# Who writes the attention mask into PSUM: two matmuls or one ScalarE copy

## What is computed

```python
q = l2norm(q) * qs; k = l2norm(k) * ksc           # then rotary tables on q and k
mask = (it < jb) | (it > jb + w) | (jb == -1)
sim = jnp.einsum('bhwie,bhwje->bhwij', bq, bk2) * QK_SCALE
sim = jnp.where(mask, -jnp.finfo(sim.dtype).max, sim)
attn = jax.nn.softmax(sim, -1)
out = jnp.einsum('bhwij,bhwje->bhwie', attn, bv2)
...
x = attn_layer(shift_tokens(x), ...) + x
x = ffn_layer(shift_tokens(x), ...) + x           # a * gelu(gate) @ W2 + b2
```

## Time and profile before

| | us |
|---|---|
| median of 3 runs | 3832.99 (3829.45 to 3838.61) |
| profiled execution, its own time | 3835.11 |
| its span, first to last instruction | 3833.3 |
| PE busy | 3290.7 (86%) |
| DVE busy | 2808.5 (73%) |
| ACT busy | 2595.7 (68%) |
| POOL busy | 2500.6 (65%) |

### The profile page before, as it was taken

One profiled execution on the slowest core, in us unless ns is written; L12 is line 12 of the kernel. 1 busy time (PEld: TensorE's weight loads), 2 busy tenths in 40 slices (PEclk: granted clock), 3 DMA queues, 4 the chain that ended last, 5 costly groups with the idle time before them and its releaser, 6 DMA issues.

```text
span 3833.3 us, 127009 instructions
## 1 busy us (share of the span) xinstructions
PE 3290.7 (86%) x52864; PEld 2810.5 (73%) x53056; DVE 2808.5 (73%) x4272; ACT 2595.7 (68%) x3787; POOL 2500.6 (65%) x2289
## 2 busy tenths in 40 slices
PE   3444448999989999899999899999999998999996
PEld 2333236888878888788888788888787887888885
DVE  5766766777777777777777777777777777777772
ACT  2222225777777777777777777777777776777774
POOL 1000007777777877777777777778777777787771
PEclk7666668999999999999999999999999999999997
DMA  1000001111111111111111111111111111111111
GB/s 56 0 0 0 0 0 35 50 41 35 35 29 40 56 34 35 35 41 41 47 35 35 34 37 59 35 35 35 35 37 55 35 35 31 41 37 30 36 34 31
DMA packets 54643, 130.05 MB, mean 34 GB/s; under 512 B 10944, under 2 KB 28864, under 8 KB 53312
## 3 DMA queue, kind: packets, MB, share of 16 engines
q1 hardware_dynamic: 54080, 122.02, 10.9%
HBM read 19.25 MB, written 2.10 MB: 6 GB/s over the span
## 4 chain that ended last, share of the span: by engine, by line
PE 72%; ACT 12%; DVE 7%; issue 7%; POOL 1%; DMA 0%; SPq 0%; ACTq 0%; DVEq 0%; POOLq 0%
PE pair L217 58%; PE pair L220 14%; ACT qT L737 7%; ACT sq L727 2%; DVE qT L362 1%; ACT ss L732 0%; DVE VA L347 0%; DVE qT L353 0%; DVE wq_l L843 0%; ACT qT L275 0%; DVE tab L835 0%; ACT qT L272 0%; DVE VB L358 0%; DVE qT L326 0%; DVE qT L316 0%
## 5 line engine op out<-in xcount | busy, mean ns | idle before, releaser
L966 POOL TENSOR_TENSOR qk<-qk,ts 128x1024 f32<-128x1024 f32 x384 | 914.8, 2383 | 312.2 <-DVE ts L857 293.4
L945 POOL TENSOR_TENSOR qk<-qk,rn 128x1024 f32<-128x1024 f32 x384 | 729.3, 1921 | 43.1 <-issue 28.3
L853 DVE TENSOR_TENSOR qk<-pair,tab 128x1024 f32<-128x1024 f32 x384 | 468.6, 1220 | 373.0 <-ACT sq L719 370.3
L217 PE MATMUL pair<-wq_h,xs_h 128*128 128x512 f32 x1152 | 515.2, 447 | 34.7 <-issue 15.0
L220 PE MATMUL pair<-small,qk 128*128 128x128 f32 x3192 | 452.5, 285 | 66.7 <-ACT qT L737 49.4
L714 ACT ACTIVATE Sx<-Sx 128x1024 f32<-128x1024 f32 x192 | 203.7, 1061 | 413.9 <-DVE Sx L870 413.9
L220 PEld LDWEIGHTS pair<-small,qk 128*128 128x128 f32 x3192 | 361.0, 146 | 151.3 <-issue 127.5
L857 DVE TENSOR_TENSOR ts<-pair,tab 128x1024 f32<-128x1024 f32 x384 | 466.5, 1215 | 0.0
L217 PE MATMUL pair<-wq_h,xs_l 128*128 128x512 f32 x1152 | 464.8, 403 | 0.0
L861 DVE TENSOR_REDUCE ss<-sq 128x16 f32<-128x1024 f32 x384 | 464.3, 1209 | 0.0
L217 PE MATMUL pair<-wq_l,xs_h 128*128 128x512 f32 x1152 | 460.8, 400 | 0.0
(11 more groups left out here) (204 smaller groups left out, 6959.1 us busy)
## 6 DMA issues: line engine op xcount, KB each, us to landing
VB<-VA SPq DMA_DIRECT2D x192, 384.0 KB, 3.5
VB<-VA SPq DMA_DIRECT2D x96, 128.0 KB, 3.4
wq_raw<-wqkv SPq DMA_DIRECT2D x6, 1536.0 KB, 8.8
xf<-xT SPq DMA_DIRECT2D x96, 64.0 KB, 1.9
xf<-xT SPq DMA_DIRECT2D x96, 63.8 KB, 2.0
wo_sb<-wo SPq DMA_DIRECT2D x6, 512.0 KB, 3.6
out<-X SPq DMA_DIRECT2D x8, 256.0 KB, 2.3
w_raw<-fw SPq DMA_DIRECT2D x6, 341.0 KB, 8.0
```

The source lines that it names most:

```text
L217: return T_.matmul(out, lhsT, rhs, start=start, stop=stop, **k)
L853: V_.tensor_tensor(h3(qk[:, now, kind, :], DH), h3(source[:, :], DH), rep(tab[:, 2 * kind, b, :], HEADS, DH), ALU.mult)
L945: G_.tensor_tensor(x, x, bc(rn[:, then, kind * HEADS:(kind + 1) * HEADS], HEADS, DH), ALU.mult).then_inc(S["scaled"], 1)
L966: G_.tensor_tensor(qk[:, now, kind, :], qk[:, now, kind, :], ts[:, kind, :], ALU.add).then_inc(S["added"], 1)
```

## The change

The bf16 mask, the bf16 identity, and the two VectorE casts that made them are gone. TensorE no longer waits for `o_kept` ahead of the scores and issues no mask matmuls; it waits for a new semaphore `masked`. ScalarE, right behind the copy of oT and ahead of the copy of kT, waits for `o_kept` and copies the f32 mask from SBUF, repeated for 8 head pairs, over all of PB. The scores still accumulate (start flag off). For that, the write flags in PB have to be set when they come: of the product of P and V only the first matmul of each bank and partition half starts a group, so that all columns are left written. At step 1, before any such product, two ordinary matmuls write PB for the same end.

```diff
-        mask_bf = sb("mask_bf", [P, BLOCKS, PAIRS * 2 * KEYS], BF16)
-        ident_bf = sb("ident_bf", [P, P], BF16)
...
                                 last = mm(PB[odd * DH:(odd + 1) * DH, to:to + WIN],
-                                          values[rows, ring, head * DH:(head + 1) * DH], PT[rows, a, q0:q0 + WIN])
+                                          values[rows, ring, head * DH:(head + 1) * DH], PT[rows, a, q0:q0 + WIN],
+                                          a == 0 and w == 0, True, skip_group_check=True)
...
             if pl.has(1):
-                if pl.has(3):
-                    e.wait_ge(S["o_kept"], blocks(pl, "o_kept", 3, 1))
                 bb = (t - 1) % BLOCKS
-                for u in range(2):
-                    mm(PB[:, u * UNIT:(u + 1) * UNIT], ident_bf[:, :], mask_bf[:, bb, u * UNIT:(u + 1) * UNIT], True, False, skip_group_check=True)
+                if t == 1:
+                    for u in range(2):
+                        last = mm(PB[:, u * UNIT:(u + 1) * UNIT], xs_h[:, 0, 0:P], wq_h[:, 0:UNIT])
+                    last.then_inc(S["opened"], 1)
+                e.wait_ge(S["masked"], blocks(pl, "masked", 1, 1))
                 e.wait_ge(S["qkT_kept"], blocks(pl, "qkT_kept", 1, 2))
...
             if pl.has(1):
+                bb = (t - 1) % BLOCKS
+                if pl.has(3):
+                    e.wait_ge(S["o_kept"], blocks(pl, "o_kept", 3, 1))
+                elif pl.has(2):
+                    e.wait_ge(S["shifted"], blocks(pl, "shifted", 2, 1))
+                else:
+                    e.wait_ge(S["opened"], 1)
+                A_.activation(h3(PB[:, :], P), rep(mask[:, bb * P:(bb + 1) * P], PAIRS, P), ACT.Copy).then_inc(S["masked"], 1)
                 e.wait_ge(S["qkT_done"], blocks(pl, "qkT_done", 1, 2))
-                bb = (t - 1) % BLOCKS
                 A_.activation(kT[:, :, WIN + bb * P:WIN + (bb + 1) * P], h3(PC[:, :], P), ACT.Copy).then_inc(S["qkT_kept"], 1)
...
             dve.wait_ge(S["loaded"], 64)
-            V_.tensor_copy(mask_bf[:, :, :].rearrange("p b (a k) -> p b a k", k=2 * KEYS),
-                           mask.rearrange("p (b o k) -> p b o k", b=BLOCKS, o=1).broadcast_to([P, BLOCKS, PAIRS, 2 * KEYS]))
-            V_.tensor_copy(ident_bf[:, :], ident)
             stage1(dve, stage1_dve)
```

More of the change, by code:

```diff
@@ L8 @@
 I32 = mybir.dt.int32
-BF16 = mybir.dt.bfloat16
 ALU = mybir.AluOpType
@@ L143, in build @@
             "seeded": 1, "newton": 3, "normed": 1, "added": 2, "scaled": 2, "qkT_done": 2, "qkT_kept": 2, "s_done": 1,
-            "maxed": 1, "shifted": 1, "exp_done": 1, "rows_summed": 1, "inverted": 1, "weighed": 1, "pT_done": 1,
+            "maxed": 1, "masked": 1, "shifted": 1, "exp_done": 1, "rows_summed": 1, "inverted": 1, "weighed": 1, "pT_done": 1,
             "pT_kept": 1, "av_done": 1, "o_kept": 1, "y_done": 1, "x_updated": 1, "v_kept": 1,
@@ L154, in build @@
         S = {n: sem(n) for n in (*STEP, *PER_SEQ, *LOADS, *PARTS, "xf0", "xf1", "vb0", "vb1", "vb2", "vb3", "phase", "loaded",
-                                 "stored", "lane0", "lane1", "lane2", "lane3", "o_copied", "o_t", "o_sum", "zeroed",
+                                 "stored", "lane0", "lane1", "lane2", "lane3", "opened", "o_copied", "o_t", "o_sum", "zeroed",
                                  "cleared", "waited")}
```

## The result

| | before | after |
|---|---|---|
| median, us | 3832.99 (5 runs) | 3856.45 (3849.24 to 3858.59, 5 runs) |
| ratio, 95% interval | | 1.0065 (1.0045 to 1.0084) |
| profiled execution, us | 3835.11 | 3849.24 |
| its span, us | 3833.3 | 3847.4 |

The forecast was 3825, with a range of 3806 to 3856.

What follows compares the result with a forecast made beforehand. The prediction took TensorE to bound the kernel: -84.5 us for the mask matmuls, +74 for odd-step stalls and +2 at layer boundaries gave about -8, so a median of 3825 us, range 3806 to 3856.

Steps and rivals of the forecast that it cites:

- What bounds the kernel: TensorE, 86% busy and 72% of the chain of waits; time taken from it counts wherever nothing else is as late.
- The odd step: Late kT copy stalls TensorE 0.76 us at the `xf` transposes, against 0.44 saved; 74 us of stalls over 94 steps.
- The even step: kT's delay is hidden at W1's third part; the 0.44 us saved is kept, narrowly, with slacks of 0.10 and 0.16.
- The second rival: ScalarE's chain from value copy to maximum bounds the even step too; at a 1.3 us mask copy 3861; chance 0.09.
- a chance of gain only: Shorter mask copy, or stalls absorbed where TensorE's issue idles let it catch up; about 3808 us; chance 0.15.
- the third rival: TensorE's clock falls after the odd step's new stall; 1.7 us in one step of four, 41 us, 3866; chance 0.13.
- The sum: Whole kernel: -84.5 for the mask matmuls, +74 for odd-step stalls, +2 at layer boundaries, giving -8.5 us.

Runs made afterwards that it cites:

- nomask: Changed kernel without any mask, neither matmuls nor ScalarE copy, so the mask is left out of the computation; 3762.24 us, ratio 0.9828.
- both: Kernel before with the ScalarE mask copy added and the mask matmuls kept; 3904.98 us, ratio 1.0215.
- swap_after: Changed kernel with the W2 product placed ahead of the `xf` transposes on TensorE; 3779.58 us, ratio 0.9866.
- kt_odd: Changed kernel with the mask copy behind the copy of kT in odd steps, ahead of it in even steps; 3783.86 us, ratio 0.9874.
- gelu64_after: Changed kernel with the three gelus cut to 64 of 256 columns and one memset more at the start; 3838.59 us, ratio 1.0025.
- even_act: Even steps as in the change (ScalarE writes the mask), odd steps as in the kernel before (two matmuls); 3825.57 us, ratio 0.9994.
- odd_act: Odd steps as in the change (ScalarE writes the mask), even steps as in the kernel before (two matmuls); 3882.72 us, ratio 1.0148.
- after_pad: Changed kernel with four semaphore increments per step on TensorE in place of the mask matmuls and their weight loads; 3862.31 us, ratio 1.0079.
- kt_first: Changed kernel with the mask copy behind the copy of kT in both kinds of step; 3792.04 us, ratio 0.9906.
- before_pad16: Kernel before with 16 semaphore increments per step on TensorE ahead of the mask matmuls; 3967.23 us, ratio 1.0355.

## Why the prediction was wrong, step by step

**What bounds the kernel:** right for the part that holds the mask matmuls, worth 0.44 us in each step (nomask: -0.43 and -0.43). It was not TensorE's path throughout: between the scores and the transposes of Q the path runs through VectorE and ScalarE, by 0.10 us, which the chain with its 72% for TensorE doesn't show. The even step failed on that piece.

**The odd step:** right. Predicted +0.32 (0.76 stalled, 0.44 saved), measured +0.34 in the median, with a stall of 0.75. Over 94 steps 74 us were predicted and 67 measured, since some steps have little or no stall. The runs both, swap_after and kt_odd show the cause: it is that kT comes late for the `xf` transposes, and nothing else of the copy.

**The even step:** this is the step that failed. The prediction said that "the even step's 0.44 is kept, narrowly", after it had checked two users of the delayed chain, the transposes of P and the square of K. The third, the transposes of Q behind the copy of P, had a slack of nothing. Measured -0.30. The term was -42 us and is -29: 13 us, which gelu64_after gives back (15.70, -15 to -18 us). The subtraction behind the maximum came 0.30 earlier against the 0.18 worked out for the maximum; with 0.18 the loss would have been larger still. The second rival named this chain, but let it decide only from a mask copy of 1.19 us. It decided at 1.03.

**What was not priced:** 15 us above the medians, in the stretch read: short idles +4.3, time at the lower clock +5.4, the long idle once per turn of the loop (blocks 9 and 10) +3.4, the rest single microseconds. The prediction put this at nothing, and had the idles as a chance of gain only, absorbed by the stall ahead of them; they grew. One of the short ones after, with the granted clock in 4 us ahead of it and in 4 us behind it:

```profile
2069.15 0.30 PE L214 MATMUL pair<-PT,VA 64*64 64x32 f32 x4 [1.22 <-issue]
```
```profile
2064.90:2068.90 4.00, 3.03 (x133) 2.75 (x132) 4.00 (x5) 3.13 (x4) 2.36 (x1) 1.00 0.02 4
2069.40:2073.40 4.00, 4.00 (x17) 3.48 (x16) 2.69 (x4) 3.00 (x3) 3.65 (x3) 0.57 0.02 4
```

That costs 1.7 us, as in the earlier trace rows. It happened behind 4 of the 14 idles of 1.15 to 1.7 us, and behind none of the 102 of 0.5 to 0.9 us, most of which are the new stall. In the window of 1900 to 2500 us the clock is 0.99 as before, and the clock loss rose by 5 us and not by 41. So the third rival in its form (the new stall as the cause in one step of four) is out.

**The sum,** over blocks 12 to 186: predicted 87 x (0.32 - 0.44) = -10 us; measured -26.1 + 29.6 = +3.5 by the medians (13.5 missed, of which 12 are the even step), +14.6 above them, 18 in all, of which 14 are left at the end of the profiled run. The other runs of after were 6 to 9 us slower than the profiled one, and of those there is no trace. The even step is thus the step that is shown to have failed, and accounts for 12 to 13 of the 31 us between the forecast and the median.

**Still open:** why the idles grow by 4 to 12 us in after, nomask, even_act, odd_act, gelu64_after and after_pad and not in swap_after, kt_odd and kt_first (34 to 37), why the two blocks at the end of the loop take most of the rest, and what else lies above the medians there. The four kernels that keep TensorE's stream as it was lie at 29.7 to 35.7 us of idles and 118.7 to 124.7 above the medians, the others but before_pad16 at 34 to 48 and 136 to 151. That a step with fewer microseconds for nearly the same instructions runs into the supply more often would fit; it wasn't shown by a run that changes the pace alone, and with one trace per kernel a difference of a few microseconds here is not safe.

## What to carry to other kernels

Work moved from the engine that bounds the kernel to one with a third of its time free costs little by its length and much by its place: the same 1.03 us copy made the kernel 0.65% slower ahead of kT, and 1.3% faster behind it in the odd steps, or with an independent product put between. When a chain is delayed, list every wait that leads back to it from the code, not the two that the trace happens to name: a wait hidden under a modelled matmul end shows no releaser, and its slack was zero. The medians of the distance from one start to another, over all steps, show such a wait. And of a gain on an engine that issues some 30 instructions a microsecond, expect a part back above the undisturbed steps; here 12 to 23 us of it, in a single trace each.

## What the hardware showed that I had not expected

ScalarE wrote 128x1024 f32 from SBUF to PSUM in 1.029 us, against 1.009 (after) and 1.028 (before) for the copy of kT the other way and 1.060 for the exp inside SBUF. The Trainium skill, "ScalarE: Activation LUTs", section "Step-by-step: what each stage is for", calls PSUM the destination of lower latency. Against the exp from SBUF to SBUF the rows agree by 0.03 us, against the copies from PSUM to SBUF they show nothing of it; no run has the same copy to both destinations.

TensorE's "issue" idles recur at the same blocks of every turn of the loop to within one block, and stand at other blocks when four instructions per step come or go (4, 5, 14, 15, 21, 22 against 1, 2, 9, 16, 24 to 26). With sixteen more semaphore increments per step, some 3% of its instructions, there were 119 such idles in place of 36, and the kernel took 3.6% longer.
